# A Flamingo block with a routed feed-forward: a block for every expert, late weight splits between the first gathers, and router logits taken from the attention's own products

## The chip, the cores and the metric

The kernel runs on one core of a Trainium2 chip. The metric is device time in microseconds (us), the slowest core's, which is here the only one. The core's engines work side by side and meet through semaphores: PE (TensorE, matmuls and transposes into PSUM, its weight loads listed as PEld), DVE (VectorE), ACT (ScalarE), POOL (GpSimd, which also issues the indirect DMAs), and SP, which issues most of the other DMAs. Each runs its instructions strictly in the order in which they are written.

## The reference, cut to what matters

```python
# x: 8 sequences x 256 tokens x 256; ctx: 8 x 120 x 128
x = x + tanh(g_xattn[0]) * L0_xattn(layernorm(x), ctx, ctx)      # one head
x = x + tanh(g_ffn[0])   * L0_ffn(layernorm(x))                  # 8 experts + 4 identity experts
x = x + tanh(g_xattn[1]) * L1_xattn(layernorm(x), ctx, ctx)      # 16 heads
x = x + tanh(g_ffn[1])   * L1_ffn(layernorm(x))                  # simulated fp8

def L0_xattn(q, k, v):
    q = q @ Wq + bq;  k = k @ Wk + bk;  v = v @ Wv + bv
    return softmax(q @ k.T) @ v

def L0_ffn(x):
    logits = x @ gate_w.T + expert_bias                # 12 logits
    top, idx = top_k(logits, 2)
    w = softmax(top) placed at idx                     # per token, 12 wide
    h = silu(x @ w1[e].T)                              # per expert e < 8, width 512
    y = h @ w2[e].T
    return sum_e w[e] * y[e] + sum(w[8:]) * x
```

## The kernel before, in words

There are 2048 tokens, in 8 batches of 256, each batch two tiles of 128 tokens. The program has three parts.

**The first stage** (to about 73 us) computes the first attention batch by batch and, from its result x1, the router's logits. Per batch, PE transposes x (`transpose_x0`), makes scores (`scores0`, against `kq`, in which keys, queries and biases are merged), transposes the probabilities and multiplies them with the values (`attend`). DVE takes means and variances of x (`stats0`), the scores' maximum (`max0_of`, whose last instruction is L1133), copies the values (`copy_v0`, L1123), adds the attention to x (`add_x1`) and takes means and variances of x1 (`stats1`). POOL turns variances into reciprocal roots (`root0`, `root1`). For the logits PE then transposes x1 (`transpose_x1`, L1802), ACT or DVE copies it (`copy_xT1`, L708 and L1154), PE multiplies it with the gate (`gate_of`, L1814), and DVE scales and adds the bias (`logits_of`, L1169). ACT also writes the normed x1 (`norm1`, L714) into a buffer that SP stores to the DRAM tensor `xn_d`. In the gaps the experts' weights (fp32, 32 chunks of 512 columns) are split into a high part (`high`, ACT, L726) and a low part (`low`, POOL L544 for 26 chunks, DVE L1160 for 6).

**Routing and the experts.** DVE picks the two best of 12 logits for each token (`highest`, `mark_highest`, `keep_first`), PE ranks the tokens within each expert, and DVE derives `slot_i`, the token of each row, and the expert of each block: 39 blocks of 128 rows, each with the rows of one expert. PE waits for all 32 splits ahead of the first block. Then each block i goes through: gather of its rows (`gather`, POOL, L579), transposes (PE, L1987), split (ACT `xh_of`, DVE `xl_of` L1358), first product (PE, L1977), tanh and gate (ACT, DVE), transposes, split, second product (PE, L1964), copy (ACT), scatter to `y_d` (POOL, L585). PE is software-pipelined: in the slot of block i it does in this order the transposes of block i+4, the first product of i+3 interleaved with the second of i, and the gate's transposes of i+2. POOL gathers six blocks ahead. The identity experts' share is added on DVE from a reload of `xn_d` (`xz`, L1389).

**The rest** (from about 230 us) gathers the two results of each token, and does the second attention and the fp8 layer.

The order on each engine is written out by hand. `own.mark` and `own.settle` are a wait of an engine for its own last instruction.

## Time and profile before

| | us |
|---|---|
| median of 3 runs (372.27, 372.34, 377.18) | 372.34 |
| profiled execution: span from first to last instruction | 378.3 |
| first stage, to the last logits | 0 to 73.4 |
| choice, ranks and slots, to the first gather | 73.4 to 87.0 |
| first product of the first block | 92.1 |
| blocks of the experts | 92 to 230 |
| gathered results, second attention, fp8 layer | 230 to 378 |

The page has no time for the profiled execution other than its span. Busy shares over the whole span are PE 92%, DVE 69%, ACT 58% and POOL 41%. In the page's 40 slices a digit is the busy share in tenths; the row PEclk is the TensorE clock that the throttle granted, and its low digits lie in the slices from 47 to 76 us and around 87 us.

### The profile page before, as it was taken

The numbers are of one execution on the slowest core, as the hardware profiler recorded it, in microseconds if no ns is written. First come the engines' busy times: TensorE is split into PE (matmuls) and PEld (weight loads), VectorE is DVE, ScalarE is ACT, GpSimd is POOL, SyncE is SP. The second block draws the span as 40 slices with busy tenths as digits, with TensorE's granted clock in tenths as the row PEclk, the third lists the DMA queues.
The fourth block names the chain that finished last, engine by engine and source line by source line (L and its number), as shares of the span: only waits on it lengthen the run. The fifth ranks groups of instructions, "written<-read, shape, count | busy, mean of one in ns | idle before, by whom it ended". The sixth has DMA issues, their size and how long they took to land.

```text
span 378.3 us, 9027 instructions
## 1 busy us (share of the span) xinstructions
PE 348.3 (92%) x2959; PEld 279.9 (74%) x2960; DVE 261.1 (69%) x659; ACT 219.8 (58%) x452; POOL 154.3 (41%) x197
## 2 busy tenths in 40 slices
PE   3997889988999999999999998879999999998995
PEld 2776769756799999999999994556676667666674
DVE  2588984685646556654554447888789888957696
ACT  2589856742444544554454452456767787774586
POOL 6279967204355556555555535412130331101100
PEclk9999975598999999999999999999999999999999
DMA  6999902221133333322322213410110100000005
GB/s 180 327 413 419 419 30 83 86 84 49 50 99 111 125 108 102 123 83 71 81 69 76 76 40 114 154 57 2 57 58 11 50 2 2 2 5 0 2 28 196
DMA packets 15386, 38.25 MB, mean 101 GB/s; under 512 B 3574, under 2 KB 4748, under 8 KB 13820
## 3 DMA queue, kind: packets, MB, share of 16 engines
q1 hardware_dynamic: 10556, 26.74, 19.5%
q0 software_dynamic: 3936, 10.45, 9.4%
q10 hardware_dynamic: 864, 0.66, 0.6%
q8 instruction: 19, 0.31, 0.3%
q14 instruction: 11, 0.09, 0.1%
HBM read 24.34 MB, written 13.50 MB: 100 GB/s over the span
## 4 chain that ended last, share of the span: by engine, by line
PE 77%; DVE 12%; ACT 5%; DMA 3%; issue 2%; POOL 0%; POOLq 0%
PE two L1964 15%; PE two L1977 14%; PE two L2113 5%; PE two L1996 4%; PE two L2143 4%; PE two L2178 4%; PE two L2099 4%; PE two L2079 3%; PE two L1814 2%; PE two L1987 2%; PE two L2170 2%; PE two L1790 1%; DVE negmax L1133 1%; DMA ident<-in_c_ident 1%; PE two L2159 1%
## 5 line engine op out<-in xcount | busy, mean ns | idle before, releaser
L1364 DVE SCALAR_TENSOR_TENSOR gate<-th,two 128x512 f32<-128x512 f32 x39 | 26.8, 688 | 58.3 <-ACT th L842 32.5
L842 ACT ACTIVATE th<-two 128x512 f32<-128x512 f32 x39 | 23.4, 599 | 71.0 <-PE two L1977 52.8
L585 POOL DMA_INDIRECT y_d<-y_sb,goal_i x39 | 38.5, 988 | 50.4 <-ACT y_sb L852 50.4
L579 POOL DMA_INDIRECT xg<-xn_d,slot_i x39 | 38.0, 974 | 32.3 <-DVE slot_i L1315 14.8
L1964 PE MATMUL two<-wh,gh 128*128 x156 | 44.2, 283 | 0.1
L1964 PE MATMUL two<-wh,gl 128*128 x156 | 44.0, 282 | 0.0
L1964 PE MATMUL two<-wl,gh 128*128 x156 | 43.8, 281 | 0.0
L599 POOL TENSOR_TENSOR rstd<-var,half 128x2 f32<-128x2 f32 x14 | 9.9, 708 | 76.7 <-DVE var L1431 76.7
L1464 DVE TENSOR_REDUCE nm<-two 128x8 f32<-128x960 f32 x32 | 36.1, 1152 | 4.5 <-PE two L2099 4.1
L544 POOL TENSOR_TENSOR wl<-wl,wh 128x512 fp32r<-128x512 f32 x26 | 34.2, 1337 | 8.1 <-ACT wh L726 8.1
L1977 PE MATMUL two<-wh,xh 128*128 x78 | 34.2, 438 | 1.4 <-DVE xl L1358 1.4
L940 ACT ACTIVATE pT<-two 120x1024 f32<-120x1024 f32 x32 | 31.1, 1038 | 7.0 <-PE two L2113 7.0
L1964 PEld LDWEIGHTS two<-wh,gh 128*128 128x128 f32 x156 | 29.5, 189 | 3.6 <-issue 0.3
L1964 PEld LDWEIGHTS two<-wl,gh 128*128 128x128 f32 x156 | 29.4, 188 | 3.3
L1964 PEld LDWEIGHTS two<-wh,gl 128*128 128x128 f32 x156 | 29.4, 188 | 3.1
L1977 PE MATMUL two<-wl,xh 128*128 x78 | 30.9, 396 | 0.0
L1977 PE MATMUL two<-wh,xl 128*128 x78 | 30.7, 394 | 0.0
L1368 DVE TENSOR_TENSOR gl<-two,gh 128x512 fp32r<-128x512 f32 x39 | 27.0, 691 | 2.6 <-ACT gh L847 1.1
L847 ACT ACTIVATE gh<-two 128x512 fp32r<-128x512 f32 x39 | 23.5, 604 | 0.1
L1996 PE MATMUL two<-ident,gate 128*128 128x128 f32 x156 | 23.3, 272 | 0.0
L726 ACT ACTIVATE wh<-wl 128x512 fp32r<-128x512 f32 x32 | 18.7, 629 | 0.0
L1996 PEld LDWEIGHTS two<-ident,gate 128*128 128x128 f32 x156 | 18.2, 141 | 0.3
(298 smaller groups left out, 883.3 us busy)
## 6 DMA issues: line engine op xcount, KB each, us to landing
wl<-in_wmoe SPq DMA_DIRECT2D x8, 1024.0 KB, 14.2
y_d<-wh SPq DMA_DIRECT2D x4, 1024.0 KB
yg<-y_d SPq DMA_DIRECT2D x7, 512.0 KB, 3.4
xn_d<-xq SPq DMA_DIRECT2D x8, 256.0 KB, 2.0
xz<-xn_d SPq DMA_DIRECT2D x8, 256.0 KB
out_x<-of SPq DMA_DIRECT2D x8, 256.0 KB, 2.0
x_sb<-in_x SPq DMA_DIRECT2D x1, 1024.0 KB, 10.1
x_sb<-in_x SPq DMA_DIRECT2D x1, 768.0 KB, 4.7
```

The costliest lines, as they stand in the source:

```text
L544: pool.tensor_tensor(wl[:, c], wl[:, c].bitcast(F32), wh[:, c], ALU.subtract).then_inc(split_l, 1)
L579: pool.indirect_dma_start(xg[:, n % 2, :], None, xn_d, bass.IndirectOffsetOnAxis(ap=slot_i[:, n:n + 1], axis=0)).then_inc(gathered[n % 2], 16)
L585: pool.indirect_dma_start(y_d, bass.IndirectOffsetOnAxis(ap=goal_i[:, n:n + 1], axis=0), y_sb[:, n % 2, :], None).then_inc(y_stored[n % 2] ...
L842: nc.scalar.activation(th[:], bank[2 + k][:], ACT.Tanh, scale=0.5).then_inc(th_ok, 1)
L847: nc.scalar.activation(gh[:, k, :], bank[4 + k][:], ACT.Copy).then_inc(gh_ok, 1)
L940: nc.scalar.activation(pT[:, r, p, :], ring(ring_of_keys(b, r) + p)[0:LK, :], ACT.Exp).then_inc(e_ok, 1)
L1364: dve.scalar_tensor_tensor(gate[:, k, :], th[:], 1.0, bank[2 + k][:], ALU.add, ALU.mult).then_inc(gate_ok, 1)
L1368: dve.tensor_tensor(gl[:, k, :], bank[4 + k][:], gh[:, k, :], ALU.subtract).then_inc(gl_ok, 1)
L1464: dve.tensor_reduce(nm[:, u, 2 * HG * p:2 * HG * (p + 1)].rearrange("p (j h) -> p j h", j=2), src.rearrange("p j (h k) -> p j h k", k=LK), ...
L1964: ins = pe.matmul(bank[6 + k][:, 0:D], (gl if part == 2 else gh)[:, k, a], (wl if part == 1 else wh)[:, bass.ds(e + (C * FF + c * D), D)], ...
L1977: ins = pe.matmul(bank[2 + k][:], (xl if part == 2 else xh)[:, k, c * P:(c + 1) * P], (wl if part == 1 else wh)[:, bass.ds(e + c * FF, FF) ...
L1996: ins = pe.transpose(bank[4 + k][:, c * P:(c + 1) * P], gate[:, k, c * P:(c + 1) * P], ident[:])
```

## The change

Four things are done together.

- **Logits without a second pass.** The centred gate is put as 12 more columns behind the keys in `kq` (`KP` = 132 instead of 120), so that `scores0` also yields x times gate; `max0_of` copies these 12 columns to `xgate`. The values get 12 more columns, values times gate (`VP` = 268), so that `attend` also yields the attention's share, which `add_x1` adds. `logits_of` only scales by `rstd1` and adds the bias. `transpose_x1`, `copy_xT1` and `gate_of` are gone. New at the start: `transpose_wv`, `copy_wvT`, `values_gate`, `values_by_gate`, `gate_bias`. Values are copied by ACT (`copy_v0`), their bias comes from a second, short matmul. The logits and the marks of the choice lie in PSUM.
- **x1 is stored raw.** Each token's row in `x_sb` and `xn_d` has 258 elements: x1, `rstd1` and `less1`. `norm1` is gone from ACT, SP stores from `x_sb`; a new DVE instruction per block, `norm_of`, norms the gathered rows ahead of PE's transposes. The reload `xz` is gone: the identity experts' share is one `tensor_scalar` on `x_sb`.
- **Every expert owns a block.** An expert's rows are rounded up to at least one block (`rows_up`, `ALU.max`); there are still 39 blocks. PE waits for the splits of experts 0 to n ahead of block n (`wait_h`) and no longer for all ahead of the first. All 32 low parts are POOL's: 23 ahead of the first gather, 9 between and behind the first six.
- **New orders** of the first stage on all engines; the negated maximum is now scaled by two `tensor_scalar` instructions; `root1` runs once for each batch.

```diff
+                    ins = dve.tensor_scalar(negmax[:, b % 2, u:u + 1], lowest[:, b % 2, u:u + 1], rstd0[:, b, u:u + 1], None,
+                                            ALU.mult)
...
             def add_x1(b):
                 dve.wait_ge(pv_done, b + 1)
...
+                for u in range(U):
+                    dve.scalar_tensor_tensor(xgate[:, b, u, :], at[:, u, D:VP], rsum[:, u:u + 1], xgate[:, b, u, :], ALU.mult,
+                                             ALU.add)
...
             def logits_of(b):
...
-                dve.wait_ge(logit_done, b + 1)
                 dve.wait_ge(rstd1_ok, root_of(b, ROOTS1))
                 for u in range(U):
-                    ins = dve.scalar_tensor_tensor(logit[:, cols(2 * b + u, E_ALL)], gate_bank(b)[:, u * GATES:u * GATES + E_ALL],
-                                                   rstd1[:, b, u:u + 1], gbias_sb[:, cols(u, E_ALL)], ALU.mult, ALU.add)
+                    ins = dve.scalar_tensor_tensor(logits[:, 2 * b + u, :], xgate[:, b, u, :], x_rstd(2 * b + u), gate_bias_at,
+                                                   ALU.mult, ALU.add)
...
+            then(dve.tensor_scalar(rows_up[:], rows_up[:], BLOCK_UP + P, None, ALU.max))
...
+            def norm_of(i, k):
+                wait(dve, gathered[k], 16 * (i + 1))
+                wait(dve, xgT_done, 2 * i + k - 1)
+                dve.tensor_scalar(xq[:, k, :], xg[:, k, 0:D], xg[:, k, D:D + 1], xg[:, k, D + 1:D + 2], ALU.mult,
+                                  ALU.add).then_inc(xq_ok, 1)
...
                 if live(i, k, 4):
                     xl_of(*ahead_of(i, k, 4))
+                if live(i, k, 5):
+                    norm_of(*ahead_of(i, k, 5))
                 if live(i, k, 3):
                     gate_of(*ahead_of(i, k, 3))
...
             def gather(n):
 
-                wait(pool, xgT_done, n - 1)
+                wait(pool, xq_ok, n - 1)
...
-            for n in range(AHEAD):
-                gather(n)
+            gather(0)
+            gather(1)
+            low(23)
+            gather(2)
+            low(24)
+            gather(3)
+            lows(25, 27)
+            gather(4)
+            low(27)
+            gather(5)
+            lows(28, CHUNKS)
...
-            pe.wait_ge(split_l, CHUNKS - len(VECTOR_LOW))
-            pe.wait_ge(split_d, len(VECTOR_LOW))
...
             def wait_h(i, k):
+                if isinstance(i, int) and 2 * i + k < E_FFN:
+                    pe.wait_ge(split_l, PER_EXPERT * (2 * i + k + 1))
```

PE at the end of the first stage, from the last batch's `attend` on. Before (`xT` is the transposed x1):

```order
L1790 MATMUL two<-v,probT 128x257 [waits x1_done,v0_ok,probT_copied]
L1790 MATMUL two<-v,probT 128x257
L1814 MATMUL two<-gate_sb,xT 128x32 [waits logit_kept,xT1_copied,exp_done]
L1814 MATMUL two<-gate_sb,xT 128x32 x3
L1802 MATMUL two<-ident,x_sb 128x128 [waits xT1_copied,x1_done]
L1802 MATMUL two<-ident,x_sb 128x128 x3
L1802 MATMUL two<-ident,x_sb 128x128 [waits xT1_copied,x1_done]
L1802 MATMUL two<-ident,x_sb 128x128 x3
```

And now, from the last but one:

```order
L1856 MATMUL two<-v,probT 128x269 [waits x1_done,v0_ok,probT_copied]
L1856 MATMUL two<-v,probT 128x269
L1846 MATMUL two<-ident,prob 120x128 [waits probT_copied,exp_done]
L1846 MATMUL two<-ident,prob 120x128
L1856 MATMUL two<-v,probT 128x269 [waits x1_done,v0_ok,probT_copied]
L1856 MATMUL two<-v,probT 128x269
L1871 MATMUL two<-ctxT_sb,wk_sb 128x480 [waits exp_done,con_in]
```

Behind the last `attend` PE now has nothing to do for the logits; L1871 belongs to the second attention.

POOL from the last roots to the first scatter (`wl` is a low part, `xg` a gathered block, `y_d` a scatter). Before:

```order
L536 TENSOR_TENSOR rstd<-var,half 128x2 [waits var1_ok]
L538 TENSOR_TENSOR less<-less,rstd 128x2 [waits pool_own]
L544 TENSOR_TENSOR wl<-wl,wh 128x512 [waits split_h]
L579 DMA xg<-xn_d,slot_i 128x256 [waits slots_kept]
L579 DMA xg<-xn_d,slot_i 128x256
L579 DMA xg<-xn_d,slot_i 128x256 [waits xgT_done] x4
L579 DMA xg<-xn_d,slot_i 128x256 [waits xgT_done,zeroed,goals_kept]
L585 DMA y_d<-y_sb,goal_i 4353x256 [waits y_kept]
```

And now:

```order
L609 DMA xg<-xn_d,slot_i 128x258
L576 TENSOR_TENSOR wl<-wl,wh 128x512 [waits split_h]
L609 DMA xg<-xn_d,slot_i 128x258 [waits xq_ok]
L576 TENSOR_TENSOR wl<-wl,wh 128x512 [waits split_h]
L609 DMA xg<-xn_d,slot_i 128x258 [waits xq_ok]
L576 TENSOR_TENSOR wl<-wl,wh 128x512 [waits split_h] x2
L609 DMA xg<-xn_d,slot_i 128x258 [waits xq_ok]
L576 TENSOR_TENSOR wl<-wl,wh 128x512 [waits split_h]
L609 DMA xg<-xn_d,slot_i 128x258 [waits xq_ok]
L576 TENSOR_TENSOR wl<-wl,wh 128x512 [waits split_h] x4
L609 DMA xg<-xn_d,slot_i 128x258 [waits xq_ok,zeroed,goals_kept]
L615 DMA y_d<-y_sb,goal_i 4353x256 [waits y_kept]
```

Nine low parts stand between the second gather and the seventh.

## Rows read from the trace of the kernel before

**Rows 1.** By stretch: length; busy us (count) of PE, PEld, DVE, ACT, POOL; granted clock; DMA.
```profile
7.00:74.00 67.00, 60.06 (x327) 49.97 (x327) 49.90 (x172) 49.05 (x114) 44.07 (x42) 0.83 0.64 249
51.00:75.00 24.00, 22.13 (x85) 19.13 (x85) 14.72 (x59) 16.18 (x37) 13.38 (x15) 0.52 0.15 59
92.00:230.00 138.00, 136.34 (x932) 124.81 (x932) 76.52 (x148) 63.72 (x154) 72.75 (x75) 1.00 0.29 86
```

**Rows 2.** Chain of waits: start, us, what; first and last of 14 PE pieces.
```profile
51.70 2.03 PE two L1790 x4
...
69.73 3.25 PE two L1814 x16
```

**Rows 3.** Timeline: start, us, what; the last x1, the last logits, the first gather.
```profile
65.66 0.88 DVE L1141 SCALAR_TENSOR_TENSOR x_sb<-two,rsum,x_sb 128x256 f32<-128x256 f32 x2
...
73.03 0.37 DVE L1169 SCALAR_TENSOR_TENSOR logit<-two,rstd,gbias_sb 128x12 f32<-128x12 f32 x2 [0.24 <-PE two L1814]
...
87.05 1.08 POOL L579 DMA_INDIRECT xg<-xn_d,slot_i  x1 [14.80 <-DVE slot_i L1315]
```

**Rows 4.** Groups by form, 0 to 92 us: busy us, mean ns of one.
```profile
L1133 DVE TENSOR_TENSOR negmax<-lowest,rstd 128x2 f32<-128x2 f32 x8 | 6.0, 747 | 0.3
L1160 DVE TENSOR_TENSOR wl<-wl,wh 128x512 fp32r<-128x512 f32 x6 | 5.7, 954 | 0.8 <-ACT wh L726 0.8
L1123 DVE SCALAR_TENSOR_TENSOR v<-two,gain,bv0g 120x256 f32<-120x256 f32 x8 | 3.8, 477 | 2.8 <-PE two L1757 2.8
L1169 DVE SCALAR_TENSOR_TENSOR logit<-two,rstd,gbias_sb 128x12 f32<-128x12 f32 x16 | 2.9, 223 | 6.5 <-PE two L1814 6.5
L1101 DVE TENSOR_SCALAR wq_sb<-wq_sb,wless 128x256 f32<-128x256 f32 x2 | 0.6, 349 | 0.0
...
L726 ACT ACTIVATE wh<-wl 128x512 fp32r<-128x512 f32 x32 | 18.7, 629 | 0.0
L714 ACT ACTIVATE xq<-x_sb,less,rstd 128x256 f32<-128x256 f32 x16 | 8.4, 589 | 0.0
L708 ACT ACTIVATE xT<-two 128x512 f32<-128x512 f32 x5 | 3.0, 598 | 5.5 <-PE two L1802 5.5
...
L544 POOL TENSOR_TENSOR wl<-wl,wh 128x512 fp32r<-128x512 f32 x26 | 34.2, 1337 | 8.1 <-ACT wh L726 8.1
L536 POOL TENSOR_TENSOR rstd<-var,half 128x2 f32<-128x2 f32 x2 | 1.8, 886 | 3.9 <-DVE var L1149 3.9
```

**Rows 5.** Timeline: POOL's roots and low parts in the first stage.
```profile
19.41 3.74 POOL L544 TENSOR_TENSOR wl<-wl,wh 128x512 fp32r<-128x512 f32 x3 [1.39 <-ACT wh L726]
...
27.43 1.64 POOL L528 TENSOR_TENSOR rstd<-var,half 128x8 f32<-128x8 f32 x1 [0.30 <-DVE var L1088]
```

**Rows 6.** Timeline: the first blocks; L579 gathers, L1987 transposes of the gathered rows.
```profile
88.43 0.96 POOL L579 DMA_INDIRECT xg<-xn_d,slot_i  x1 [0.31 <-issue]
...
91.14 0.20 PEld L1987 LDWEIGHTS two<-ident,xg 128*128 128x128 f32 x2 [0.38 <-DMA xg<-xn_d,slot_i]
...
99.44 0.38 PE L1987 MATMUL two<-ident,xg 128*128 128x128 f32 x2
...
106.40 0.38 PE L1987 MATMUL two<-ident,xg 128*128 128x128 f32 x2
```

**Rows 7.** Timeline: the steady run of the blocks.
```profile
111.91 0.97 POOL L579 DMA_INDIRECT xg<-xn_d,slot_i  x1 [0.30 <-issue]
...
115.33 0.97 POOL L579 DMA_INDIRECT xg<-xn_d,slot_i  x1 [0.30 <-issue]
...
115.28 0.42 DVE L1358 TENSOR_TENSOR xl<-two,xh 128x256 fp32r<-128x256 f32 x1
...
116.83 0.38 PE L1987 MATMUL two<-ident,xg 128*128 128x128 f32 x2
```

**Rows 8.** Timeline: a tensor_scalar on DVE while POOL issues a gather.
```profile
94.82 0.94 POOL L579 DMA_INDIRECT xg<-xn_d,slot_i  x1 [1.36 <-PE two L1987]
...
95.00 0.17 DVE L1339 TENSOR_SCALAR dif<-ex 128x16 f32<-128x16 f32 x1
```

More of the change, by code:

```diff
@@ L28 @@
 TILES = B * U
+XP = D + 2
+KP = LK + 12
+VP = D + 12
 C = D // P
@@ L45 @@
 NB = 4
-NX = 4
 HG = HEADS // NB
@@ L345, in build @@
             "of_ok")
+        x_in = [sem(f"x_in{k}") for k in range(4)]
         chunk_in = [sem(f"chunk_in{k}") for k in range(LOADS)]
@@ L540, in low, with lows @@
-            def low(j):
-                pool.wait_ge(split_h, j + 1)
-                c = cols(j, CHUNK)
+                pool.tensor_tensor(less, less1[:].rearrange("p b u -> p (b u)")[:, t], rstd, ALU.mult).then_inc(rstd1_ok, 1)
+            def low(n):
+                pool.wait_ge(split_h, n + 1)
+                c = cols(n, CHUNK)
                 pool.tensor_tensor(wl[:, c], wl[:, c].bitcast(F32), wh[:, c], ALU.subtract).then_inc(split_l, 1)
+            def lows(lo, hi):
+                for n in range(lo, hi):
+                    low(n)
@@ L564, in _ @@
+            lows(6, 9)
             root1(1)
-            low(25)
-            low(27)
+            lows(9, 12)
             root1(2)
-            for j in range(28, 30):
-                low(j)
+            lows(12, 15)
             root1(3)
-            low(30)
+            lows(15, 17)
             root1(4)
-            low(31)
+            lows(17, 19)
+            root1(5)
+            low(19)
+            root1(6)
+            root1(7)
+            lows(20, 23)
             pool.wait_ge(slots_kept, 1)
@@ L726, in high, with highs @@
                 nc.scalar.activation(wh[:, c], wl[:, c].bitcast(F32), ACT.Copy).then_inc(split_h, 1)
+            def highs(lo, hi):
+                for n in range(lo, hi):
+                    high(n)
+            def highs(lo, hi):
+                for n in range(lo, hi):
+                    high(n)
             copy_wkT()
+            copy_xT(0)
+            spread_std(0)
             gains_of()
-            copy_xT(0)
+            two_ones()
             copy_merged()
             copy_keys(0)
+            copy_wvT()
@@ L750, in _ @@
[L750 to L764 removed]
+            spread_std(1)
+            copy_keys(3)
+            high(2)
+            spread_std(2)
@@ new lines, in _ @@
+            high(3)
+            exp0_of(0)
+            copy_v0(0)
+            spread_std(3)
+            high(4)
+            copy_probT(0)
+            copy_keys(4)
+            copy_xT(2)
+            exp0_of(1)
+            high(5)
+            copy_v0(1)
+            high(6)
+            high(7)
+            spread_std(4)
+            copy_probT(1)
+            copy_keys(5)
+            copy_xT(3)
+            exp0_of(2)
+            high(8)
+            high(9)
+            spread_std(5)
@@ L769, in _ @@
[L769 removed]
+            exp0_of(5)
+            copy_v0(5)
             high(16)
[L771 removed]
+            high(17)
+            high(18)
+            copy_probT(5)
             copy_xT(7)
[L773 to L783 removed]
@@ L1385, in pair_xz @@
                     slot(i, k)
-                    if k == 0:
-                        wait_apart(dve, xz_in, 16 * i, dve_tick)
-                    t = 2 * i + (k - 2)
-                    ins = dve.scalar_tensor_tensor(x_sb[:, cols(t, D)], xz[:, k * D:(k + 1) * D], cz[:, cols(t, 1)],
-                                                   x_sb[:, cols(t, D)], ALU.mult, ALU.add)
-                ins.then_inc(xz_used, 1)
-            slot(-2, 0)
-            scale_of_wf()
+                    t = 2 * i + (k - 4)
+                    dve.tensor_scalar(x_tile(t), x_tile(t), keep_x[:, cols(t, 1)], add_x[:, cols(t, 1)], ALU.mult, ALU.add)
+            norm_of(0, 0)
+            norm_of(0, 1)
+            xl_of(0, 0)
             slot(-2, 1)
-            weights()
             pair(-1)
-            pair(0)
-            with dve.Fori(1, B + 1) as i:
+            for n, (i, k) in enumerate(((0, 0), (0, 1), (1, 0), (1, 1))):
+                slot(i, k)
+                if n < 3:
+                    weights(n)
+                else:
+                    scale_of_wf()
+            with dve.Fori(2, B + 2) as i:
                 pair_xz(i)
-            with dve.Fori(B + 1, PAIRS - 3) as i:
+            with dve.Fori(B + 2, PAIRS - 3) as i:
                 pair(i)
@@ L2031, in _ @@
                 mix(s // 2, s % 2, None, e)
-            pair(0)
-            with pe.Fori(1, PAIRS - 3) as i:
+            for i in range(3):
+                pair(i)
+            with pe.Fori(3, PAIRS - 3) as i:
                 pair(i)
```

617 lines of the change are left out of this document (278 added, 339 removed).

## The prediction

> **What bounds the kernel now.** I read the busy time by stretch first [rows 1]. From 92 to 230 us PE is busy in 136.3 of 138 us: the blocks are bound by PE, at the full clock, and no instruction of PE is taken from a block. From 7 to 74 us no engine is full: PE 60.1, DVE 49.9, ACT 49.1, POOL 44.1 of 67 us. That is a stage of chains between engines, and it is where the change works. From 51 to 75 us the granted clock is 0.52, which is the lower of TensorE's two levels, 1.2 GHz, for nearly all of that stretch. The chain of waits runs through PE there: 14 pieces from the `attend` at 51.70 us to the last gate product at 69.73 us [rows 2], 20.0 us together. The timeline [rows 3] shows the end: x1 is complete at 66.5 us, the last logits at 73.4, the first gather at 87.05. So 6.9 us pass between x1 and the logits, and 13.6 in the choice, the ranks and the slots.
>
> **Which time the sum is made against.** The span is 378.3 us, 6.0 above the median of 372.34; the three runs are two at 372.3 and one at 377.2. At the full clock the 20.0 us of chain pieces would be up to 10 us shorter. My reading, not shown by a row, is that most of the 6.0 us is this half clock, and that the median run gets its last logits at about 73.4 - 6.0 = 67.4 us. I take the first stage's gain from 67.4 and keep 73.4 as the other end.
>
> **First stage, what goes.** The transposes of x1, their copies and the gate products leave PE's queue, so that nothing of PE lies behind the last `attend`. DVE loses L1133 in its old form 6.0, six low parts 5.7, eight value copies 3.8 [rows 4], and three copies like L708's at 0.6, so 1.8: 17.3 us. It gains 16 small additions like L1169 at 0.22 (3.6), 16 scalings of the maximum at the 0.17 of L1339 [rows 8] (2.7), 8 short copies at the same price (1.4) and about 1.7 at the start: 9.4. Its 49.9 become 42.0. ACT loses 8.4 and 3.0 [rows 4] and gains 8 value copies, at DVE's 0.48 at most 3.8: 49.1 become 41.5, of which 12 high parts (7.0) come only behind the last probabilities. I read L1133 as paying for company: 747 ns for two elements, against 169 ns for sixteen in L1339.
>
> **First stage, what is then late.** POOL. `logits_of` waits on DVE for `root1`, which now stands behind low parts, once per batch. Ahead of the last root lie 20 low parts at 3.74 / 3 = 1.25 us [rows 5], 25.0; two further roots of x at 1.64 [rows 5] and their products, 3.6; eight roots at 0.89 [rows 4] which with product and hand-over I take as 1.2, 9.6. That is 38.2 us from the 19.4 us of the first low part, so 57.6, and 0.4 for the logits: 58.0. DVE's 42.0 from 7 us on would end at 49, ACT sooner. For waits that are not in these sums I add 1: last logits at **59.0**, a gain of **8.4**. The bounds: if only the end behind x1 is shortened (6.9 us to 1.3 for statistics and 1.2 + 0.4 for root and logits, some 3 to 4 us), the gain is 3.5; if the median run has the profile's clock and the new stage meets POOL's sum, it is 73.4 - 58.0 = 15.4. The value lies nearer the low half since the profile's clock is not the median's by my reading.
>
> **Choice and routing.** The same chain of DVE instructions, now on PSUM, and one more of 8 elements (`ALU.max`): +0.2. Keeping 39 blocks, the empty expert's block costs nothing: PE always ran 39.
>
> **First block.** `norm_of` comes between the gather and the transposes; the row nearest to it is L1101, 349 ns for the same 128x256 [rows 4]. PE's filling matmuls cover a part: +0.2 (0 to 0.5). The earlier start that the split waits would allow is worth nothing, because the 32 low parts were finished long ahead of the first product: POOL had been idle for 14.8 us when it issued the first gather [rows 3], 5 us ahead of that product. The deferral frees POOL at a time when POOL waits anyway, and is paid for in the next item.
>
> **The first gathers.** Behind gather 1 (88.43 + 0.96 = 89.4) [rows 6] POOL now has nine low parts (11.3) and four gathers with their gaps (0.97 + 0.30 each [rows 7], 5.1) ahead of gather 6: it starts at 105.8 on the old time scale. A gather's rows are there 2.7 us behind its start (88.43 to 91.14) [rows 6], the norm takes 0.35: 108.9. PE wanted these rows at 106.40 [rows 6]. So **+2.5**. Later gathers catch up, as POOL needs 2.3 us for a gather and a scatter and PE 3.47 for a slot. The bounds: +1.5 if PE is held elsewhere and the waits overlap, +4.5 if the low parts take the 1.34 of their mean [rows 4] and block 4 is late too.
>
> **The blocks.** `norm_of` stands on DVE ahead of `gate_of`. In the steady run the gather of block i+5 starts at 111.91 and has landed by 114.6; DVE comes to the norm behind `xl_of`, at 115.7; it would end at 116.05, and PE transposes at 116.83 [rows 7]. 0.8 us of slack: cost 0, covered by PE's own work. DVE has room (76.5 of 138 busy, and 39 norms add 13.6). Without the cover, each 0.1 us beyond the slack costs some 3.6 us over 36 blocks. At 115.7 POOL is issuing a gather (115.33 to 116.30) [rows 7]; the trace has a `tensor_scalar` at 95.00 that took its 0.17 us within a gather's issue of 94.82 to 95.76 [rows 8], so I charge no wait, though 16 elements are a weak witness for 256. The Trainium skill (SBUF — State Buffer, "Who interferes with whom") speaks against the change here: a `tensor_scalar` between two SBUF tensors can run in a mode that takes the port pair shared with GpSimd, and whoever is second waits for the whole instruction. By that rule the norm would begin at 116.30 and end at 116.65, still 0.2 ahead of PE, so that the sum stays and only the slack shrinks.
>
> **The rest.** Same instructions on a stride of 258 instead of 256: 0.
>
> **Sum.** -8.4 + 0.2 + 0.2 + 2.5 = -5.5 us: 372.3 - 5.5 = **366.8**. Made against the profiled execution with its half clock kept, last logits at about 61: 378.3 - 12.4 + 2.9 = 368.8, which is the same figure within what I know.
>
> **The rivals.** A measurement of this kernel tells about 2% from no change: bounds 364.9 and 379.8.
>
> - Forecast, 0.40: 364 to 370.
> - *More of the stage was clock and crowding than I allow*, 0.36. For it: at 0.52 clock the chain was PE's [rows 1, 2], and all of that second pass is gone. Then the stage gives 11 to 15: 372.3 - 12.5 + 2.9 = 362.7, from 357 to 364.9. Against it: POOL's sum.
> - *The chain stays*, 0.12: scores, maximum, probabilities, `attend`, x1 set the pace of a batch as before, the unloaded engines only wait longer, and the tail alone is saved: 372.3 - 3.5 + 2.9 = 371.7, 370 to 374. This is also the case in which the change does less than it says.
> - *The clock falls earlier*, 0.06, since PE has less to do between its waits: from 51 to 75 us PE was busy for 22.1 us at the lower level [rows 1]; with about a third gone as the second pass, 15 us are left for the last three batches, which at the full clock are about half. So up to +8 if the fall comes three batches ahead of the end: 366.8 + 8 = 375, 372 to 379.
> - *The norm starves PE* (the other side), 0.06: gather, norm and transposes form a loop through scatter and `y_sb`, with 0.8 us of slack, 0.2 if the norm waits for POOL. It decides against the change when the norm is late by more than 13.0 / 36 = 0.36 us in every slot; at 0.5 us it gives 366.8 + 18 = 385. For it: rows of 1032 bytes could land later, and the norm also holds up `gate_of`. Against it: the 2.7 us of [rows 6].
>
> The second rival and the lower edge of the forecast, 0.04, lie below 364.9: faster 0.40. The last gives slower 0.06, the rest 0.54. The range leaves out the last rival and the bottom of the second: 359 to 373.
>
> **What would show it.** In the changed profile: last logits at 59 us (57 to 62), with `logits_of` waiting for POOL's roots; no wait of DVE's scaling near 0.7 us; the first gather 13.8 us behind them; low parts between the first gathers, and PE's one stall of 2 to 3 us at the transposes of block 6; PE busy above 98% from there to the end of the blocks, at 3.47 us a slot. The prediction is wrong if the last logits are outside 57 to 62, if the stall is absent or is repeated in later slots, or if the granted clock falls ahead of 45 us.

## The result, and the profile of the changed kernel

The changed kernel takes 375.23 us (median of 20 runs, 372.91 to 378.77), the kernel before 376.81 us (median of 20, 371.35 to 380.75). The ratio is 1.0062, 95% interval 1.0038 to 1.0087: no difference by the 2% bound, and within it slightly slower. The kernel before has runs near 372 us and runs near 377 and above, which is why its median over all 20 lies above the changed kernel's, while the ratio, which leaves out for each kernel the runs more than 1.5% above its fastest, lies above 1. My 366.8 us and my range to 373 were both too low.

The stretches of the changed kernel, in the columns of [rows 1]:

```profile
7.00:74.00 67.00, 57.86 (x326) 43.48 (x326) 51.81 (x222) 47.27 (x114) 40.21 (x47) 0.95 0.71 269
51.00:75.00 24.00, 17.51 (x102) 12.11 (x101) 20.61 (x79) 13.64 (x32) 9.93 (x12) 0.86 0.21 69
92.00:230.00 138.00, 134.83 (x909) 122.57 (x910) 90.28 (x188) 60.96 (x148) 74.09 (x77) 0.99 0.25 69
```

The granted clock from 51 to 75 us is 0.86, where it was 0.52. DVE has 90.3 us of work beside the blocks in place of 76.5: the 39 norms. The timeline (start, us, what) at the places of [rows 3] and [rows 6]; L1386 is `norm_of`, L576 a low part, L609 a gather, L2015 the transposes:

```profile
60.35 0.37 DVE L1208 SCALAR_TENSOR_TENSOR two<-xgate,x_sb,two 128x12 f32<-128x12 f32 x2 [1.09 <-POOL x_sb L570]
75.17 1.08 POOL L609 DMA_INDIRECT xg<-xn_d,slot_i  x1 [11.19 <-DVE slot_i L1336]
...
79.35 0.41 DVE L1386 TENSOR_SCALAR xq<-xg 128x256 f32<-128x256 f32 x1 [0.35 <-DMA xg<-xn_d,slot_i]
82.09 3.24 DVE L1386 TENSOR_SCALAR xq<-xg 128x256 f32<-128x256 f32 x1 [0.95 <-DMA xg<-xn_d,slot_i]
86.86 1.16 DVE L1386 TENSOR_SCALAR xq<-xg 128x256 f32<-128x256 f32 x1
90.72 3.67 DVE L1386 TENSOR_SCALAR xq<-xg 128x256 f32<-128x256 f32 x1
95.85 0.40 DVE L1386 TENSOR_SCALAR xq<-xg 128x256 f32<-128x256 f32 x1
...
82.67 2.49 POOL L576 TENSOR_TENSOR wl<-wl,wh 128x512 fp32r<-128x512 f32 x2
86.57 1.30 POOL L576 TENSOR_TENSOR wl<-wl,wh 128x512 fp32r<-128x512 f32 x1
89.29 4.95 POOL L576 TENSOR_TENSOR wl<-wl,wh 128x512 fp32r<-128x512 f32 x4
...
85.38 0.69 PE L2015 MATMUL two<-ident,xq 128*128 128x128 f32 x2 [2.97 <-DVE xq L1386]
94.45 0.44 PE L2015 MATMUL two<-ident,xq 128*128 128x128 f32 x2 [3.45 <-DVE xq L1386]
103.11 0.38 PE L2015 MATMUL two<-ident,xq 128*128 128x128 f32 x2
```

Read it by its ends. The norms of 3.24, 1.16 and 3.67 us end at 85.33, 88.02 and 94.39; the groups of low parts end at 85.16, 87.87 and 94.24, each 0.15 or 0.17 us earlier. The same instruction takes 0.41 us at 79.35 and 0.40 at 95.85, where no low part runs. One thing in these rows does not fit a plain hold: the norm of 82.09 started 0.58 us ahead of its low parts (82.67), which is more than the 0.41 us of a free norm, and yet it was held. In the repeat below it is the same (80.06 and 80.60). PE waits for it 2.97 and 3.45 us, 7.0 in all. The last line is block 6: the first gather came 11.9 us earlier than in [rows 3], block 6's transposes only 3.3 us earlier than in [rows 6].

### The profile page after: what moved, and what is told of

It reads as the page before. It is cut to its first block, busy times and chain, and to the rows that moved or that the text cites. A ratio compares the mean times of both kernels' runs of the same rounds, so it can differ in the third digit from the quotient of the medians.

```text
span 376.9 us, 8952 instructions
## 1 busy us (share of the span) xinstructions
PE 340.6 (90%) x2887; PEld 268.1 (71%) x2888; DVE 273.4 (73%) x723; ACT 212.5 (56%) x441; POOL 161.8 (43%) x211
## 4 chain that ended last, share of the span: by engine, by line
PE 73%; DVE 11%; ACT 7%; DMA 4%; issue 2%; POOL 1%; SPq 0%; DVEq 0%; ACTq 0%
PE two L1990 15%; PE two L2005 14%; PE two L2142 5%; PE two L2172 4%; PE two L2024 4%; PE two L2207 4%; PE two L2128 4%; PE two L2108 3%; PE two L2015 2%; DVE xq L1386 2%; DMA x_sb<-in_x 2%; PE two L2199 2%; PE two L1874 1%; PE two L2188 1%; PE two L1856 1%
## 5 line engine op out<-in xcount | busy, mean ns | idle before, releaser
L609 POOL DMA_INDIRECT xg<-xn_d,slot_i x39 | 38.0, 975 | 23.6 <-DVE slot_i L1336 11.2
L576 POOL TENSOR_TENSOR wl<-wl,wh 128x512 fp32r<-128x512 f32 x32 | 40.1, 1274 | 0.1
L2005 PE MATMUL two<-wl,xh 128*128 x78 | 31.7, 407 | 0.0
L2005 PE MATMUL two<-wh,xl 128*128 x78 | 31.5, 403 | 0.0
L1386 DVE TENSOR_SCALAR xq<-xg 128x256 f32<-128x256 f32 x39 | 23.1, 592 | 4.9 <-DMA xg<-xn_d,slot_i 4.9
L2015 PE MATMUL two<-ident,xq 128*128 128x128 f32 x78 | 15.3, 279 | 7.0 <-DVE xq L1386 7.0
```

What stands on the lines that cost most here:

```text
L576: pool.tensor_tensor(wl[:, c], wl[:, c].bitcast(F32), wh[:, c], ALU.subtract).then_inc(split_l, 1)
L609: pool.indirect_dma_start(xg[:, n % 2, :], None, xn_d, bass.IndirectOffsetOnAxis(ap=slot_i[:, n:n + 1], axis=0)).then_inc(gathered[n % 2], 16)
L1386: dve.tensor_scalar(xq[:, k, :], xg[:, k, 0:D], xg[:, k, D:D + 1], xg[:, k, D + 1:D + 2], ALU.mult, ALU.add).then_inc(xq_ok, 1)
L2005: ins = pe.matmul(bank[2 + k][:], (xl if part == 2 else xh)[:, k, c * P:(c + 1) * P], (wl if part == 1 else wh)[:, bass.ds(e + c * FF, FF) ...
```

## The experiments

Ten edits of the changed kernel, and a second profile of each of the two kernels. "Median" is over all runs. "Ratio" is against the kernel before on the same chip; the kernels were measured on several chips, so two of them are compared by their ratios. "Ranks" is the time from the end of the last logits to the first gather, "start" that from the first gather to block 6's transposes, both in the profiled execution.

| kernel | median us (runs) | ratio, interval | ranks | start |
|---|---|---|---|---|
| before, first profile | 376.81 (20) | 1 | 13.65 | 19.35 |
| before, again | 371.82 (1) | | 13.41 | 19.32 |
| changed | 375.23 (20) | 1.0062, 1.0038 to 1.0087 | 14.45 | 27.94 |
| changed, again | 377.66 (12) | 1.0093, 1.0051 to 1.0135 | 14.26 | 27.94 |
| low parts first | 374.75 (12) | 1.0055, 1.0019 to 1.0090 | 20.65 | 18.91 |
| norm as scalar_tensor_tensor | 376.92 (6) | 1.0113, 1.0057 to 1.0169 | 14.63 | 28.48 |
| both of these | 376.02 (6) | 1.0102, 1.0049 to 1.0154 | 20.64 | 19.19 |
| norm on ACT | 371.90 (12) | 0.9949, 0.9905 to 0.9993 | 14.67 | 22.00 |
| norm on ACT, low parts first | 372.31 (12) | 0.9993, 0.9958 to 1.0028 | 20.63 | 18.62 |
| norm on ACT, new order | 369.24 (12) | 0.9884, 0.9846 to 0.9923 | 14.18 | 18.63 |
| norm on ACT, second new order | 369.45 (6) | 0.9893, 0.9843 to 0.9943 | 13.96 | 18.72 |
| norm on DVE, second new order | 373.07 (12) | 0.9992, 0.9956 to 1.0029 | 14.67 | 23.62 |
| short low parts | 367.66 (4) | 0.9886, 0.9837 to 0.9935 | 13.91 | 19.85 |
| norm in halves | 381.10 (4) | 1.0132, 1.0074 to 1.0191 | 16.91 | 28.46 |

**Low parts first.**

```diff
-            lows(20, 23)
+            lows(20, CHUNKS)
             pool.wait_ge(slots_kept, 1)
...
-            gather(0)
-            gather(1)
-            low(23)
-            gather(2)
...
-            gather(5)
-            lows(28, CHUNKS)
+            for n in range(AHEAD):
+                gather(n)
```

> The changed kernel with all 32 low parts ahead of the first gather and the six gathers back to back behind it, as before the change. Theory A (DVE's norm can't finish while POOL runs low parts, so the low parts between the gathers hold it for 3.2, 1.2 and 3.7 us and PE waits 7.0 us on xq): the nine low parts end at 64.0 + 9 x 1.25 = 75.2 us, the first gather starts at 75 to 76 us, every norm takes 0.4 us, PE's waits on xq between the first gather and block 6 fall from 7.0 us to under 1, and the transposes of block 6 come at 96 to 97 us in place of 103.1; the kernel is 6 to 7 us faster than the changed one, near 369 us. Theory B (POOL's order only makes gathers late, the norm is not held): the gathers come earlier, but the transposes of block 6 gain 2 to 3 us at most, near 372.5. Theory C (holding goes both ways: any DVE instruction with its inputs in SBUF is slowed by a low part): the low parts now lie beside the choice and the ranks; the first gather slips by 2 us or more, and half of A's gain is lost, near 372.

The norms and PE's waits came out as theory A has it, the first gather as C has it, only dearer than C's 2 us. Two answers, of the norm's line from 70 to 130 us (count, ns min/median/max) and of DVE's groups from 62 to 78 us (busy us, mean ns):

```profile
L1377 DVE TENSOR_SCALAR xq<-xg x16: 403/406/414, 82.2 to 128.0; 128x256 f32<-128x256 f32 x16
...
L1315 DVE TENSOR_TENSOR onecol<-cols_are,col 128x1248 f16<-128x1248 f16 x1 | 1.8, 1754 | 0.0
L1299 DVE SCALAR_TENSOR_TENSOR ahead<-rows_up,before 128x64 f32<-128x64 f32 x1 | 1.2, 1247 | 0.0
...
L1298 DVE TENSOR_SCALAR rows_up<-rows_up 128x8 f32<-128x8 f32 x1 | 1.1, 1109 | 0.0
...
L1304 DVE TENSOR_REDUCE pos<-prod 128x32 f32<-128x288 f32 x1 | 0.5, 453 | 0.0
...
L1301 DVE TENSOR_TENSOR place<-first,two 128x128 f32<-128x128 f32 x1 | 0.3, 286 | 0.0
```

and the same instructions in the changed kernel, where POOL was idle beside them:

```profile
L1324 DVE TENSOR_TENSOR onecol<-cols_are,col 128x1248 f16<-128x1248 f16 x1 | 0.8, 807 | 0.0
...
L1313 DVE TENSOR_REDUCE pos<-prod 128x32 f32<-128x288 f32 x1 | 0.5, 452 | 0.0
...
L1310 DVE TENSOR_TENSOR place<-first,two 128x128 f32<-128x128 f32 x1 | 0.3, 289 | 0.0
L1308 DVE SCALAR_TENSOR_TENSOR ahead<-rows_up,before 128x64 f32<-128x64 f32 x1 | 0.2, 226 | 0.0
```

Held are the instructions with two inputs in SBUF and the `tensor_scalar` from SBUF to SBUF. Not held are the reductions and whatever takes a tensor from PSUM (`two`). Eight instructions are longer by 6.5 us together (onecol 0.95, `dif` 1.07, `ahead` 1.02, `col` 1.01, `rows_up` 0.94, the two products 0.69 and 0.42, `up` 0.46), and the ranks last 6.2 us longer. So the low parts took from the ranks what they gave back to the norms: the start is 9.0 us shorter, and 6.2 of it are gone before it. The Trainium skill (SBUF — State Buffer, "Who interferes with whom") has this very list: two SBUF inputs or a 2-port mode contend with GpSimd, a `tensor_reduce` never does on trn2. The trace agrees (reduction 453 and 452 ns, `ahead` 1247 and 226). Theory A's 369 us and C's 372 were both missed (374.75): the ranks lost three times what C had allowed.

**Norm as scalar_tensor_tensor.**

```diff
-                dve.tensor_scalar(xq[:, k, :], xg[:, k, 0:D], xg[:, k, D:D + 1], xg[:, k, D + 1:D + 2], ALU.mult, ALU.add)
+                dve.scalar_tensor_tensor(xq[:, k, :], xg[:, k, 0:D], xg[:, k, D:D + 1],
+                                         xg[:, k, D + 1:D + 2].to_broadcast([P, D]), ALU.mult, ALU.add)
```

> The changed kernel, low parts between the gathers as in it, but the norm is written as a scalar_tensor_tensor (same two operations, the mean as a broadcast second tensor). Theory A in its narrow form (it is tensor_scalar's mode between two SBUF tensors that is held): each norm takes 0.45 us, also beside low parts, PE's waits on xq fall from 7.0 us to under 1, the kernel gains 5 to 7 us, 368 to 370. Theory C (any DVE instruction that reads two SBUF tensors is held by a low part): the three long norms stay within 20% of 3.2, 1.2 and 3.7 us, and the time stays within 1 us of 375.2. Theory B: norms short, but the transposes of block 6 still at 101 us or later.

The norm's line and who waited for it:

```profile
L1386 DVE SCALAR_TENSOR_TENSOR xq<-xg x15: 469/479/3980, 76.5 to 128.8; 128x256 f32<-128x256 f32 x15
...
  PE two L2015: 7.5, 4
```

Still held, 3.98 us at most, PE's waits 7.5 us. The narrow form of A has fallen, C holds: this form, with two tensors in SBUF, is held like the `tensor_scalar`, which has one. A form with one input in SBUF that is not a `tensor_scalar` was not tried, so that the edit does not show whether it could go free.

**Both.** The two edits above together.

> Both edits: all 32 low parts ahead of the first gather, and the norm as a scalar_tensor_tensor. Theory A: nothing is left for the second edit to remove, so the same as the kernel with the low parts first within 1 us (near 369), unless the new form is longer in each slot: at 0.45 for 0.40 us, inside the slack of 0.8 us, 0. Theory B: the same, near 372.5.

The start is 19.19 us against 18.91 with the low parts first alone, PE's waits 1.1 us against 0.6. So the second edit added nothing where no low part met it, as A says. Its absolute time was off for the same reason as above: the ranks, 20.64 us. The ratio, 1.0102, can't be told from 1.0055.

**Norm on ACT.** The first lines are ACT's `slot`; DVE's `norm_of` is taken out.

```diff
             def slot(i, k):
                 if live(i, k, 4):
                     xh_of(*ahead_of(i, k, 4))
+                if live(i, k, 5):
+                    norm_of(*ahead_of(i, k, 5))
...
+                nc.scalar.activation(xq[:, k, :], xg[:, k, 0:D], ACT.Identity, scale=xg[:, k, D:D + 1],
+                                     bias=xg[:, k, D + 1:D + 2]).then_inc(xq_ok, 1)
```

> The changed kernel, low parts between the gathers as in it, but the norm runs on ACT (one activation with scale and bias behind xh, 0.38 us, where ACT waits 1.5 to 2.4 us a slot for PE). Theories A and C (a low part holds DVE, not ACT): the norms take 0.4 us, PE's waits on xq fall from 7.0 us to under 1.5, block 6's transposes at 96 to 98 us, 5 to 7 us faster than the changed kernel: 368 to 370. Theory B (late gathers): block 6's transposes stay at 101 us or later, 373 to 375.

The norm's line, PE's waits, and the stall at block 6 with the low parts that stand ahead of its gather:

```profile
L878 ACT ACTIVATE xq<-xg x17: 592/602/605, 76.2 to 128.1; 128x256 f32<-128x256 f32 x17
...
  PE two L2014: 4.0, 5
...
86.63 5.03 POOL L576 TENSOR_TENSOR wl<-wl,wh 128x512 fp32r<-128x512 f32 x4
91.82 0.97 POOL L609 DMA_INDIRECT xg<-xn_d,slot_i  x1 [0.16 <-issue]
...
95.28 0.44 PE L2014 MATMUL two<-ident,xq 128*128 128x128 f32 x2 [1.39 <-ACT xq L878]
```

No norm is held beside the same low parts, and the start falls from 27.94 to 22.00 us. The time falls by about 1.1% (0.9949 against 1.0062, each against before), some 4 us; I had forecast 5 to 7. ACT's norm takes 0.60 us, not the 0.4 that I expected. What is left is theory B's share: late gathers, 4.0 us of PE's waits, with the stall that I had forecast for block 6. B was right about that part, 22.00 - 19.35 = 2.65 us, and wrong about the larger one.

**The kernel before, again.** Unchanged.

> The kernel before, unchanged, for a second profile: what lies between its times near 372 us and near 377. Theory P (my reading in the prediction: the profile of before is of a slower run because of its clock from 51 to 75 us): if this execution lasts 371 to 373 us, its granted clock from 51 to 75 us is 0.9 or more in place of 0.52, its last logits come at 67 to 68 us in place of 73.4 and the first gather at 81 in place of 87.05. Theory Q (the difference is made elsewhere): at 371 to 373 us the last logits still come at 72 to 74 us, and the 6 us are missing behind them. If it lasts near 377 again, its stretches should repeat those of the first profile, and nothing is told apart.

The stretch from 51 to 75 us in the columns of [rows 1], and the timeline at the places of [rows 3] and [rows 6]:

```profile
51.00:75.00 24.00, 19.62 (x125) 15.51 (x125) 22.14 (x80) 19.89 (x45) 13.66 (x15) 1.00 0.28 99
```

```profile
64.48 0.37 DVE L1169 SCALAR_TENSOR_TENSOR logit<-two,rstd,gbias_sb 128x12 f32<-128x12 f32 x2 [0.16 <-POOL less L538]
...
78.26 1.08 POOL L579 DMA_INDIRECT xg<-xn_d,slot_i  x1 [12.65 <-DVE slot_i L1315]
...
97.58 0.38 PE L1987 MATMUL two<-ident,xg 128*128 128x128 f32 x2
```

Theory P holds in kind. At a granted clock of 1.00 the last logits end at 64.85 us in place of 73.40, and the whole span is 370.0 in place of 378.3: 8.6 us there, 8.3 at the end, so all of the difference is made in this stretch. The size of P's figure was off: 64.85, not 67.4. The reason is that I had taken a median from a span. A run's time is longer than its span from first to last instruction: here 371.82 and 370.0, in every run of this kernel on record by 1.8 to 1.9 us. The first profile, with its span of 378.3, was thus an execution of some 380.1 us, 7.8 above the median and not 6.0. The logits here wait 0.16 us for POOL; at half clock they waited for PE.

**The changed kernel, again.** Unchanged.

> The changed kernel, unchanged, for a second profile and on one chip with the others. Its profiled execution of 378.77 us had its last logits at 60.72 us and the first gather at 75.17, while its first stage in the variants of it came at 58.1 to 58.9 and 73.0 to 73.3. Theory D (every execution pays the held norms; the first 2 us are what differs between executions): first gather at 73.0 to 73.5, three norms of 3.2, 1.2 and 3.7 us within 10%, PE's waits on xq 6.5 to 7.5 us, block 6's transposes 27.5 to 28.3 us behind the first gather, 374 to 376 us. If the held norms were a chance of that one profile, they are below 1 us here.

```profile
58.48 0.37 DVE L1208 SCALAR_TENSOR_TENSOR two<-xgate,x_sb,two 128x12 f32<-128x12 f32 x2 [1.09 <-POOL x_sb L570]
...
73.11 1.08 POOL L609 DMA_INDIRECT xg<-xn_d,slot_i  x1 [11.00 <-DVE slot_i L1336]
...
88.58 3.74 DVE L1386 TENSOR_SCALAR xq<-xg 128x256 f32<-128x256 f32 x1
...
101.05 0.38 PE L2015 MATMUL two<-ident,xq 128*128 128x128 f32 x2
```

Theory D holds: start 27.94 us again, PE's waits 7.0 again. Only the time, a median of 377.66, lies above its 374 to 376. With the two repeats the balance can be made between two executions that are alike, before (370.0 us) against changed (374.2): last logits -6.0, first gather -5.15, block 6's transposes +3.5, the load of the results (224.48 and 228.71) +4.2, end +4.2.

**New order of POOL, norm on ACT.**

```diff
-            lows(20, 23)
+            lows(20, 24)
             pool.wait_ge(slots_kept, 1)
...
+            for n in range(4):
+                gather(n)
+            low(24)
+            gather(4)
+            low(25)
+            gather(5)
+            lows(26, 28)
+            gather(6)
+            lows(28, CHUNKS)
```

> The norm on ACT, and POOL's order changed: low part 23 ahead of the first gather, gathers 0 to 3 back to back, then one low part, gather 4, one, gather 5, two, gather 6, and the last four behind gather 6. With the norm on ACT alone PE still waited 4.0 us on xq, 2.6 of it at blocks 1 to 4 and 1.39 at block 6, whose gather stood behind four low parts. Theory A (what is left there is late gathers): those waits fall to under 1.5 us, block 6's transposes come 18.9 to 20 us behind the first gather in place of 22.0, and the time falls by 2 to 3 us against the norm on ACT alone, to 369 or 370. Rival: the waits only move (the gather of block 6 is early, but the low parts behind it hold up scatter 0 and gather 7, whose rows block 7 wants 3.5 us later): no gain, 372.

The start is 18.63 us, the waits on xq 1.2: A's part came out, and with 0.9884 this is the fastest kernel that computes everything, 1.2% below the one before. The rival came out too. Gather 7 behind the last four low parts, ACT's norm of it, and block 7's transposes:

```profile
94.24 0.97 POOL L609 DMA_INDIRECT xg<-xn_d,slot_i  x1 [0.31 <-issue]
...
97.83 0.60 ACT L876 ACTIVATE xq<-xg 128x256 f32<-128x256 f32 x1 [5.08 <-DMA xg<-xn_d,slot_i]
...
98.48 0.44 PE L2012 MATMUL two<-ident,xq 128*128 128x128 f32 x2 [0.55 <-issue]
```

Block 7 follows block 6 (91.58) by 6.9 us in place of 3.47, so 3.2 of the 3.7 us that block 6 had gained on the norm on ACT alone are lost one block later. The two profiles are then almost equal, 367.6 and 368.0 us. The ratios are 2.4 us apart (0.9884 and 0.9949), on two chips and with intervals that overlap, so that a gain of this order over the norm on ACT alone is not shown by the traces.

**Norm on ACT, low parts first.** The first and the fourth edit together.

> The norm on ACT with all 32 low parts ahead of the first gather. Theory A with C (low parts hold DVE's instructions that read SBUF, wherever they meet): the ranks and slots are held as in the kernel with low parts first, 20 to 21 us from the last logits to the first gather in place of 14.4; the blocks start free; since no low part meets a norm there, ACT gains nothing over DVE: the same time as with the norm on DVE and low parts first, 374 to 375. If ACT's norm is better for another reason than the low parts, it is near 371.

Ranks 20.63 and start 18.62 us, as with the norm on DVE (20.65 and 18.91): A with C holds for the stretch that it speaks of. The time, 0.9993 against 1.0055, was better than forecast. In the profiles this lies behind the blocks: from the load of the results to the end 145.6 us here and 148.4 there, where the granted clock from 245 to 260 us was 0.77. What makes that fall stays open (below).

**Second new order, norm on ACT.** Behind gather 6 two low parts, scatter 0, gather 7, two low parts, scatter 1.

```diff
             gather(6)
-            lows(28, CHUNKS)
+            lows(28, 30)
+            scatter(0)
+            gather(7)
+            lows(30, CHUNKS)
+            scatter(1)
```

> As the kernel with the norm on ACT and the new order of POOL, but behind gather 6 only two low parts, then scatter 0 and gather 7, then the last two low parts and scatter 1. There gather 7 had been issued at 94.24, its norm began at 97.83 and PE lost 2.3 and 0.55 us. Theory A: gather 7 is issued at 91.6 to 92.9, PE's waits of 2.3 and 0.55 us disappear, block 7's transposes come 3.5 us behind block 6's in place of 6.9, and the time falls by 2 to 3 us, to 366 to 367. Rival: the wait moves on to gather 8 or to scatter 1, less than 1 us gained, 368.5 to 369.

The rival was right. The waits of 2.3 and 0.55 us are gone and block 7's transposes come 4.0 us behind block 6's, but blocks 8 to 11 follow at 4.7, 3.7, 4.2 and 4.0 us; block 11 is reached at 111.85 against 112.61, 0.46 of which was there at the first gather, and the time is the same (0.9893 and 0.9884). This profile has one more row that bears on the hold. `cw` has 32 elements and takes a usual 0.23 us:

```profile
92.74 2.16 DVE L1377 TENSOR_SCALAR cw<-wval,gain 128x32 f32<-128x32 f32 x1
...
92.31 2.54 POOL L576 TENSOR_TENSOR wl<-wl,wh 128x512 fp32r<-128x512 f32 x2
```

It ends at 94.90, 0.05 behind the second low part: a short instruction, too, can be held over two of them.

**Second new order, norm on DVE.** The same order in the changed kernel.

> The same new order of POOL as the first of these, but the norm stays on DVE. Theory A: the norms of blocks 0 and 1 have no low part beside them any more; those of blocks 2 to 7 meet one or two back to back and are held 0.5 to 2 us, none for 3 us or more, since no more than two low parts stand together; PE's waits on xq up to block 7 fall from 7.0 to 3 to 5 us; 371 to 373 us, that is 4 to 6 us behind the same order with the norm on ACT. Rival (only the order mattered): within 1 us of the norm on ACT.

PE's waits are 4.7 us and the time is 373.07: 3.6 us behind the same order with the norm on ACT, on the same chip, just under what A gave. The rival, within 1 us, has fallen, and A holds in kind. Its lengths were too small: three norms, each beside two low parts, took 2.40, 2.51 and 2.85 us, where A gave 2 at most. One norm and the low parts of its time:

```profile
94.52 2.85 DVE L1388 TENSOR_SCALAR xq<-xg 128x256 f32<-128x256 f32 x1
94.71 2.50 POOL L576 TENSOR_TENSOR wl<-wl,wh 128x512 fp32r<-128x512 f32 x2
```

The norm started 0.19 us ahead of the low parts and was held all the same, until 97.37, 0.16 behind their end. By the Trainium skill (SBUF — State Buffer, "Who interferes with whom") whoever issues first gets the ports for the whole instruction. This row does not show that advantage, nor do the norms of 82.09 in the changed kernel and 80.06 in its repeat, which started 0.58 and 0.54 us ahead. The recorded start may lie ahead of the moment at which the instruction takes the port; no run shows it.

**Short low parts.** The nine low parts between the gathers compute 16 of 512 columns, so the rest of those parts is missing and the kernel's result is not the reference's; it serves for its times alone.

```diff
+                c = slice(n * CHUNK, n * CHUNK + 16)
+                pool.tensor_tensor(wl[:, c], wl[:, c].bitcast(F32), wh[:, c], ALU.subtract).then_inc(split_l, 1)
...
-            low(23)
+            low_short(23)
```

> The changed kernel with the nine low parts that stand between the gathers cut to 16 of their 512 columns (the rest of those parts of the weights is not computed): same instructions, same order, same waits, only shorter on POOL. Theory A (it is the low parts' running time that holds the norm): all norms within 0.7 us, PE's waits on xq from 7.0 to under 1.5, block 6's transposes 18.9 to 20 us behind the first gather in place of 27.94, 367 to 369 us. Rival (the gathers' issue on POOL, or the waits of the order itself, hold it): norms of over 1 us remain beside the gathers, and block 6 comes 22 us or more behind the first gather.

```profile
L1396 DVE TENSOR_SCALAR xq<-xg x15: 402/404/414, 75.4 to 119.1; 128x256 f32<-128x256 f32 x15
...
83.73 0.76 POOL L582 TENSOR_TENSOR wl<-wl,wh 128x16 fp32r<-128x16 f32 x4
```

Theory A to the number: same order, same waits, the longest norm of these 414 ns, PE's waits 0.3 us, start 19.85 us. It is the running time of the low parts that holds the norm. The gathers are all still there, and the norms that run within one take their usual 0.41 us. No norm here starts within a gather less than 0.6 us ahead of a low part, as the one of 82.09 did in the changed kernel, so that case stays open.

**Norm in halves.**

```diff
+                for h in (slice(0, P), slice(P, D)):
+                    ins = dve.tensor_scalar(xq[:, k, h], xg[:, k, h], xg[:, k, D:D + 1], xg[:, k, D + 1:D + 2], ALU.mult, ALU.add)
+                ins.then_inc(xq_ok, 1)
```

> The changed kernel with the norm as two instructions of 128 elements in place of one of 256. In the norm first on the port the low parts can't interrupt it; in a queue of low parts DVE might get its turn between two of them. If DVE gets a turn at each boundary (as the instructions of the ranks did when low parts ran beside them, each held 0.6 to 1.25 us): each half is held one low part at most, the long norms shrink from 3.2 and 3.7 us to 2.0 to 2.6, PE's waits from 7.0 to 4 to 5 us. If DVE is held until the group of low parts is over, whatever its size: the first half takes about 3.0 and 3.5 us, the second 0.25, their sum within 0.3 us of the one norm's, PE's waits 7.0 to 7.5 us, and the two instructions add 0.1 us to each slot, inside the slack: 375 to 378 us.

```profile
86.05 3.42 DVE L1387 TENSOR_SCALAR xq<-xg 128x128 f32<-128x128 f32 x2 [0.94 <-DMA xg<-xn_d,slot_i]
...
95.24 3.71 DVE L1387 TENSOR_SCALAR xq<-xg 128x128 f32<-128x128 f32 x2
```

DVE got no turn between low parts: both halves together end at 89.47 and 98.95, 0.35 behind the groups' ends at 89.12 and 98.60. Taken singly, the first halves last 3.17 and 3.45 us, to 0.09 behind the groups' ends, and the second ones 0.33. The second theory holds, though PE's waits are 6.3 us and not 7.0 to 7.5. Its first gather came only at 78.93 us, in a first stage that the edit does not touch, so its absolute time is not read.

## Why the prediction was wrong, point by point

**Which time the sum is made against.** Half right. What lay between profile and median was indeed the half clock from 51 to 75 us, and the repeat shows it. But the 6.0 us came from a span set against a time; span against span it is 8.3, and at the last logits 8.6, so the place to subtract from was 64.85, not 67.4. The gain of the first stage was 6.0 us, not 8.4, for an end that I had right.

**First stage.** The figure was right, the reason only in part. Forecast 59.0, with `logits_of` waiting for POOL's roots; measured 58.85, with 1.09 us of waiting for POOL. But I had POOL as the engine that sets the pace, with 38.2 us of work behind its first low part. In the repeat this work is 34.9 us (25.0 for the 20 low parts as forecast, some 0.95 and not 1.2 for each of the eight roots, 2.5 and not 3.6 for the two of x), and POOL waits 3.9 us between, 2.0 of them ahead of the last root, for DVE's variance of the last x1:

```profile
57.47 0.70 POOL L568 TENSOR_TENSOR x_sb<-var,half 128x2 f32<-128x2 f32 x1 [2.04 <-DVE var L1200]
```

So at the end x1 came last and not POOL; roots counted too dear and waits counted too low cancelled to within 0.2 us, which is luck. In ten profiles with this stage the last logits end between 58.1 and 59.2 us, in the other two at 60.72 (the first) and 62.02 (the halves). The rival "the chain stays" has fallen, and so has "the clock falls earlier": in both profiles of the changed kernel the granted clock was 1.00 to 60 us. It was 0.77 in 60 to 75, which "more of the stage was clock" did not foresee; that rival was the true description of the first profile of before (73.40 to 60.72, 12.7 us) and not of its faster runs.

**Choice and routing.** Forecast +0.2, measured +0.8 (13.65 to 14.45; 13.41 to 14.26 in the repeats). In the repeats 0.7 of it is that DVE waits longer for PE (0.67 and 0.25 us against 0.22). Three low parts still run beside the choice (58.40 to 62.12 in the repeat) and hold nothing there: its instructions, with a tensor in PSUM, take 0.36 or 0.37 us beside them and behind them.

**First gathers.** The mechanism was right and the size nearly so: +2.5 forecast, 2.65 with the norm out of the way. It showed at block 6 (1.39 us) and in small waits at blocks 1 to 4. In the changed kernel itself the one stall that I had named at block 6 is absent: PE stands at blocks 2 and 4 (2.97 and 3.45 us). And 2.65 is taken against the kernel before, as the forecast was; against the same norm on ACT with all gathers early (18.62) the late gathers cost 3.4.

**The norm in the first blocks: the step that failed.** I charged +0.2 us for `norm_of` in the first block, 0 in the others, and wrote "I charge no wait". The runs show 5.9 us (27.94 against 22.00). Against the short low parts it is 8.1 us with the late gathers (19.85). Two errors made it. First, I took the norm's slack in the steady run, where POOL only gathers and scatters, for the whole of the blocks, and did not lay the nine low parts, which I had counted in the paragraph before, beside the norms of the same 20 us. Second, the witness in [rows 8] had the wrong partner: a gather's issue. That reading of the row was right, since gathers hold nothing here (411 ns median in the steady run). The right witness stood in [rows 4]: L1133, two elements, both inputs in SBUF, 747 ns, which I read as "company" and followed no further. Its eight instances took 161 to 1133 ns, and the seven long ones end within 0.03 us of a low part's end. In the changed kernel its successor scales one element at a time, and goes free (204 to 215 ns) beside low parts too:

```profile
L1179 DVE TENSOR_SCALAR negmax<-lowest,rstd 128x1 f32<-128x1 f32 x16 | 2.7, 210 | 0.0
```

The rule of the Trainium skill (SBUF — State Buffer, "Who interferes with whom") that I weighed was the right rule; I applied it to the gather alone. It gives a wait for the other's whole instruction; here the norm waited for two and three of them.

**The blocks.** Forecast 0. From block 6's transposes to the load of the results 126.9 us before and 127.7 changed, in the repeats: +0.8, as some slots take 3.5 to 3.8 us in place of 3.47. "The norm starves PE" in every slot did not come.

**The sum again with what was measured**, on the repeats: -6.0 + 0.85 + 8.6 (19.32 to 27.94) + 0.8 = +4.2 us, and the spans differ by 374.2 - 370.0 = 4.2. From the forecast's -5.5 that is 9.7 us: 5.9 the first gathers and norms, 2.4 the time subtracted from, 0.65 the choice and 0.8 the blocks. By the ratios of the table it is +0.6% (2.3 us) and, in the repeat, +0.9% (3.5 us).

**What hid the sign.** In the first pair of profiles the change looks 1.4 us better, since before ran there at half clock. No term of that difference belongs to the moved work.

## What to carry to other kernels

When work on GpSimd is moved into a gap, list what VectorE does in that gap, and sort it: two SBUF inputs or a `tensor_scalar` from SBUF to SBUF (of 8 elements and more; that of one element was not) was held here until GpSimd's instruction, or a whole group of them, was over; a reduction or an operand in PSUM was not. Such work has two homes that these runs show: a stretch in which VectorE works from PSUM (here the choice of experts, some 4 us), and another engine for the held instruction (ACT took 0.60 us for it in place of 0.40, and the kernel was 4 us faster). A third, pieces so small that nobody waits, is only suggested by the short low parts; the whole work was not tried in such pieces. And before a gain is subtracted from a profile, check that the profile is of the run that the median stands for, span against span: one stretch at the lower clock moved this one by 8 us.

## What the runs showed of the hardware that I had not expected

- The hold is not always one instruction long. The last three of four low parts back to back held one norm for 3.67 us and two halves for 3.71; the norm ended 0.15 us behind the last.
- The instructions of the ranks did get through between low parts (`dif` 1.24 us, one low part's 1.25), the norm never did. Length does not decide it: the 32 elements of `cw` were held over two low parts, and in the first profile of before DVE's own low part of 512 columns (L1160, 37.75 to 39.56) got through behind one. All that were held over a boundary, the norm in its forms and `cw`, take a factor from SBUF; those that got through have constants or none. No run tries this, so why stays open.
- An indirect gather's issue on POOL (0.97 us) did not lengthen a norm that ran within it: 0.41 us at 79.35 beside the gather of 79.27.
- ACT's norm, 0.60 us, is longer than DVE's 0.40, with the same 128x256.
- DVE's norm takes 0.40 us for 256 elements and, free, 0.33 for 128, so 128 elements more cost 0.07 us. From PSUM the step from 256 (`xl_of`, 0.42) to 512 (`gate_of`, 0.69) costs 0.26, about twice as much for an element.
- The granted clock in 245 to 260 us was 1.00 in both profiles of before and in all four kernels with the norm on ACT, and 0.77 to 0.89 in four of the eight with the norm on DVE (changed, low parts first, scalar_tensor_tensor, both). The changed kernel's repeat had 1.00. It costs 1.2 us at 0.89 and 2.9 at 0.77 of the stretch from the load of the results to the end (145.5, 146.7 and 148.4). Its cause was not tried.
- The half clock from 51 to 75 us does not explain every longer time of the kernel before. The nine runs on record whose mean granted clock is that of its first profile, 0.964, took 380.5 to 381.3 us; those near 377 have 0.979 to 0.998, where half the clock over these 24 us alone would leave 0.97. What makes those near 377, and what decides over the clock, is open.
